# A four-layer graph network with expert layers: streams of constant products in nineteen places of TensorE's program

## The reference

```python
edge_index = jnp.stack([src, dst])
x = x + _L0_gnn_ref(_layernorm(x), edge_index, ...)     # mean over neighbours, 2 products, batch norm, relu
x = x + _L0_ffn_ref(_layernorm(x)[None], ...)[0]        # causal attention, 8 experts, softmax gate
x = x + _L1_gnn_ref(_layernorm(x), edge_index, ...)     # 2 masked attention layers, 2 batch norms each
x = x + _L1_ffn_ref(_layernorm(x)[None], ...)[0]        # 8 experts, top 2, inner width 1024
x = x + _L2_gnn_ref(_layernorm(x), edge_index, ...)     # 4 bases, weights by node, row norm
x = x + _L2_ffn_ref(_layernorm(x)[None], ...)[0]        # 8 experts, top 2, inner width 128
x = x + _L3_gnn_ref(_layernorm(x), edge_index, ...)     # normalised convolution, batch norm, gelu
x = x + _L3_ffn_ref(_layernorm(x)[None], ...)[0]        # 8 experts, top 2, gated, inner width 1536
```

## Time and profile before

| | |
|---|---|
| median of 3 runs | 1766.1 us (1761.97 to 1770.35) |
| the profiled execution's own time | 1765.15 us |
| its span | 1763.3 us |
| TensorE busy | 1551.2 us, 88% of the span |
| VectorE busy | 1252.9 us, 71% |
| ScalarE busy | 936.8 us, 53% |
| mean granted TensorE clock over the span | 0.933 of full speed |

### The profile page before, as it was taken

How to read it: one execution, slowest core, us unless ns; L and a number is a source line. 1 busy time by engine, 2 the same in 40 slices (tenths; PEclk the granted TensorE clock), 3 DMA queues, 4 the chain that set the end, 5 groups by cost and what they waited for, 6 DMA issues and landing times. The chain is left out here.

```text
span 1763.3 us, 25730 instructions
## 1 busy us (share of the span) xinstructions
PE 1551.2 (88%) x8459; PEld 1243.9 (71%) x8459; DVE 1252.9 (71%) x2075; ACT 936.8 (53%) x1590; POOL 248.5 (14%) x250
## 2 busy tenths in 40 slices
PE   6687999998996999568999957798689999999998
PEld 6667766786884887446878835584478888888886
DVE  7863664247574476558999967444579999999998
ACT  1123355433561364126999825431258878778774
POOL 2200542001120022023000030100072000000003
PEclk9988899899998999868999979799889999999999
DMA  9001000003101001224683140001325508955003
GB/s 306 28 1 48 1 1 1 13 1 132 49 2 36 1 1 62 96 64 144 243 316 137 39 157 1 0 1 71 145 71 233 232 24 327 364 225 232 18 20 98
DMA packets 42461, 173.57 MB, mean 98 GB/s; under 512 B 10219, under 2 KB 10472, under 8 KB 26905
## 3 DMA queue, kind: packets, MB, share of 16 engines
q1 hardware_dynamic: 28822, 153.94, 23.2%
q0 software_dynamic: 8960, 10.29, 2.2%
q10 hardware_dynamic: 4608, 8.39, 1.2%
HBM read 275.74 MB, written 19.51 MB: 167 GB/s over the span
## 5 line engine op out<-in xcount | busy, mean ns | idle before, releaser
L665 POOL DMA_INDIRECT sb_W<-slots_out,sb_slus x20 | 27.6, 1382 | 609.7 <-DMA slots_out<-sb_rC 604.2
L1388 ACT ACTIVATE sb_rF<-sb_rF,sb_nmx 125x625 f32<-125x625 f32 (+4 forms) x120 | 89.5, 746 | 45.0 <-DVE sb_nmx L1886 44.9
L357 DVE TENSOR_TENSOR sb_rA_r<-sb_W,sb_rA_r 128x1024 fp32r<-128x1024 f32 x68 | 83.3, 1225 | 12.2 <-ACT sb_rA_r L1487 12.2
L614 POOL TENSOR_TENSOR sb_rstd<-sb_ve,sb_half 125x5 f32<-125x5 f32 (+1 forms) x17 | 19.0, 1116 | 513.9 <-DVE sb_ve L1807 248.0
L736 PE MATMUL bank<-sb_ident,sb_XN 125*128 125x125 f32 x160 | 31.2, 382 | 65.0 <-DVE sb_XN L1833 65.0
L1886 DVE CUSTOM_DVE_ANT_0 sb_rF<-bank,sb_rG 125x625 f32<-125x625 f32 x80 | 61.5, 807 | 36.0 <-PE bank L833 35.2
L357 DVE TENSOR_TENSOR sb_XT_r<-sb_W,sb_XT_r 128x1024 fp32r<-128x1024 f32 x68 | 82.8, 1218 | 0.1
L357 DVE TENSOR_TENSOR sb_rB_r<-sb_W,sb_rB_r 128x1024 fp32r<-128x1024 f32 x68 | 82.8, 1218 | 0.0
L1487 ACT ACTIVATE sb_rA_r<-sb_W 128x1024 fp32r<-128x1024 f32 x68 | 71.4, 1050 | 17.8 <-DMA sb_W<-in_w_m 15.3
L1129 PE MATMUL bank<-sb_rA 125*125 125x313 bf16 x400 | 60.5, 315 | 21.9 <-DVE sb_rA L2212 18.7
L736 PEld LDWEIGHTS bank<-sb_ident,sb_XN 125*128 125x128 f32 x160 | 29.0, 208 | 67.4 <-DVE sb_XN L1833 67.3
(11 more groups left out here) (497 smaller groups left out, 4873.2 us busy)
## 6 DMA issues: line engine op xcount, KB each, us to landing
sb_W<-in_w_m SPq DMA_DIRECT2D x204, 1024.0 KB
sb_rDE<-in_w_m SPq DMA_DIRECT2D x17, 1024.0 KB
sb_rC<-slots_in SPq DMA_DIRECT2D x34, 256.0 KB, 2.7
sb_W<-in_w_g SPq DMA_DIRECT2D x8, 1024.0 KB, 4.9
slots_out<-sb_rC ACTq DMA_DIRECT2D x32, 256.0 KB, 2.1
slots_in<-sb_rC SPq DMA_DIRECT2D x1, 4608.0 KB, 14.4
sb_W<-in_w_a SPq DMA_DIRECT2D x4, 1024.0 KB, 30.5
sb_W<-in_w_m SPq DMA_DIRECT2D x2, 2048.0 KB, 18.6
```

Of the source, the lines that this page charges most:

```text
L357: eng.tensor_tensor(lo, src[:, HALF * h:HALF * (h + 1)], hi.bitcast(F32), ALU.subtract).then_inc(split(r, p, h, b, "lo")[0], 1)
L614: pool.tensor_tensor(dst, src, half8[0:src.shape[0], :].broadcast_to([src.shape[0], k]), ALU.pow).then_inc(S("pow"), 1)
L665: pool.indirect_dma_start(out=G[r][k][:, t], out_offset=None, in_=YS[0:P * KEPT], in_offset=bass.IndirectOffsetOnAxis(ap=slus[:, k, t:t + ...
L1388: act.activation(SM[:, s % 4, 0:kn], SM[:, s % 4, 0:kn], ACT.Exp, scale=-1.0, bias=nmx[:, s:s + 1], accum_out=dens[:, s:s + 1]).then_inc(S ...
```

## The change

A function `keep(b, n)` is added. It issues n float32 products of `ones` (128x128) with one column of `ones` repeated over 512 columns into bank b. Nobody reads the result. It is called in nineteen places of the program's course (15 calls in the code, some in a loop or a function called several times), 112 products in all, always where TensorE's next instruction waits for another engine. Because the stream writes a bank, four of the calls have a wait of their own in front that says the bank has been read: `h_done` for the batch norms, `ag_done` in graph layer 2. In the diff the first call stands in `routed_feats` (expert layers 1, 2 and 3), the second in the first block of `block_loop(1)`, and the two behind `project` in the loop over graph layer 1's two attention layers.

```diff
+            def keep(b, n):
+                for _ in range(n):
+                    pe.matmul(bank[:, b, :], ones[:], ones[:, 0:1].broadcast_to([P, D]), start=True, stop=True)
...
                 logit_rows(r)
+                keep(5, 4)
...
                         pe.wait_ge(S("b2_done"), T)
                         turn(0, b)
+                        keep(7, 4)
                         nodes(b + 1)
...
+            pe.wait_ge(S("h_done"), 8)
+            keep(7, 3)
             to_rows(HB, S("rows_full"), S("bn_out"), 0)
+            keep(7, 2)
...
+            keep(7, 3)
             pe.wait_ge(S("msk_act"), 2 * T)
...
             mixture(0)
+            keep(5 + (UNITS - 1) % 3, 7)
             ln_to_feats(3)
...
                 project([(Wo, OT)], S("g_wo_full"))
                 pe.wait_ge(S("ld_gf"), layer * 16 + 16)
+                pe.wait_ge(S("h_done"), layer * 16 + 16)
+                keep(7, 3)
...
+                pe.wait_ge(S("h_done"), layer * 16 + 24)
+                keep(7, 6)
                 pe.wait_ge(S("g_x2"), layer * 2 + 2)
                 pe.wait_ge(S("g_x2v"), layer * 2 + 2)
             to_rows(XT, S("rows_full"))
+            keep(7, 14)
...
             block_loop(1)
+            keep(7, 15)
             ln_to_feats(5)
...
+            pe.wait_ge(S("ag_done"), 9)
+            keep(0, 17)
             routed_feats(6, 7, 2)
...
             mixture(2)
+            keep(5 + (UNITS - 1) % 3, 3)
...
+            pe.wait_ge(S("h_done"), LAYERS * 16 + 16)
+            keep(7, 4)
             to_rows(HB, S("rows_full"), S("bn_out"), 4)
+            keep(7, 6)
             routed_feats(8, 9, 3)
             feats_ready(9)
             slots(3)
+            keep(5, 4)
             block_loop(3)
```

## The result

The changed kernel takes 1744.3 us (median of 4 runs, 1743.42 to 1746.73) against 1768.2 us for the kernel before (4 runs, 1761.97 to 1771.53): a ratio of 0.987, 95% interval 0.985 to 0.989. The forecast was 1742 us. On two other chips the changed kernel took 1746.3 and 1746.8 us, at ratios of 0.989 and 0.990.

What follows compares the result with a forecast made beforehand. Work at half clock behind TensorE's pauses was taken to stand on the path; halving its time where waited for summed to 23.0 us, so 1765.15 - 23.0 = 1742.2 us. Own range 1733 to 1752; 1728 to 1757 holds 8 in 10.

Steps and rivals of the forecast that it cites:

- The price of a product: Each product of the added streams: taken as 0.87 us at full clock, bounded above by some 1.75 us at half clock.
- the idle times left: Pauses filled by streams: 3.5 us left at expert layer 1, 1.8 behind `block_loop(1)`, 2.7 behind graph layer 2.
- Rests of 2.5 to 3.5 us as an even chance: Idle rests around streams: up to 1.9 us counted as keeping the clock, 2.5 to 3.5 us an even chance or worse.
- Graph layer 1: Inner products behind its pauses: full instead of half clock saves 2.4 us in the first layer, 3.0 in the second.
- The next layer's products: Graph layer 1, behind the second batch norm: mean gain 1.9 us, 1.0 if the clock falls ahead of the stream.
- Graph layer 0, 4.6 us: Graph layer 0 into attention 0: 25 transposes save 1.9 us, tiny products and transposes 2.0, `heads` 0.7.
- Expert layer 1, 1.9 us: Expert layer 1: `slots` ahead of `block_loop(1)` 1.0 us, that loop's second block 0.6, gate 0.3.
- `first_nodes` gives nothing, since the second block waits: Ahead of `block_loop(1)`: no gain from `first_nodes`, as the second block waits for GpSimd's and the DMAs' way through HBM.
- Expert layer 2 and the last loop: Expert layer 2's transposes 0.8 us at four in ten, first products of `router(2)` 1.7, ahead of the last loop 3.9.
- The first rival: All streams hold the clock and every chance becomes one: 33 us gained, 1732 us; chance 0.17.
- the second (1757): The clock falls in the rests all the same; only rests of 1.6 us and less pay: 8 us, 1757 us; chance 0.10.
- the third: The stream itself is slow, constants not counted as work or repeated column streaming badly: 1830 or 1797 us; chance 0.06.

Runs made afterwards that it cites:

- the run with the earlier start: Against the changed kernel, the stream of graph layer 1's second batch norm writes the first bank, starts at once and has 8 products instead of 6: 1746.6 us.

## Why the prediction was right, and where it wasn't

The mechanism held throughout: half clock behind pauses was the cost, the streams run at full clock, and only work that is waited for gave something. The last block loop is unchanged, as said. Against the terms of the sum:

- **The price of a product**, 0.87 us: right. The three longest streams show it, thirty records in 13.09 us (0.87 us a product) behind `block_loop(1)`, and the idle times left are those of the list:

```profile
743.62 3.61 PE L747 MATMUL bank<-sb_ones 128*128 128x512 f32 x8
750.70 1.51 PE L736 MATMUL bank<-sb_ident,sb_XN 125*128 125x125 f32 x6 [3.46 <-DVE sb_XN L1858]
...
1014.10 13.09 PE L747 MATMUL bank<-sb_ones 128*128 128x512 f32 x30
1029.38 4.03 PE L736 MATMUL bank<-sb_ident,sb_XN 125*128 125x125 f32 x20 [2.18 <-DVE sb_XN L1858]
...
1077.87 14.92 PE L747 MATMUL bank<-sb_ones 128*128 128x512 f32 x34
1095.44 2.47 PE L736 MATMUL bank<-sb_ident,sb_XN 125*128 125x125 f32 x20 [2.65 <-DVE sb_XN L1858]
```

  3.46, 2.18 and 2.65 us, for 3.5, 1.8 and 2.7 expected.
- **Rests of 2.5 to 3.5 us as an even chance**: right as a chance. 3.46 and 2.18 us were followed by a fall, 2.65 wasn't; of the two rests of 2.5 us ahead of the streams in graph layer 1's second batch norms the first was (565.63), the second wasn't. Over the three traces of the changed kernel, two of the six rests of 2.5 us were followed by a fall, none of the three of 2.65 (the same rest was in the run with the earlier start), and all three of 3.46. Between 1.9 and 2.5 us I had no price; the one rest there in the first trace, 2.18 us, was followed by a fall.
- **Graph layer 1**: 2.3 us for the first inner products (2.4 said) and 2.9 for the second (3.0). The next layer's products gave 3.1 and began 2.1 us late: 1.0, the figure given for a fall there. The mean of 1.9 was of the two cases; the first trace has the lower. In the second trace of the changed kernel the clock held there, and from the inner products to the next layer it took 17.3 us instead of 19.0, the 1.7 us that the prediction gave for the fall.
- **Graph layer 0, 4.6 us**: the term that failed. The transposes gave 1.6 (1.9 said), all the rest 0.6 instead of 2.7: the rest of 1.7 us and the tiny products behind it didn't hold, the clock fell at 176.5 us in them, and the products at 184.07 ran at 0.55. I priced 2.7 of it against the text's own reservation that I "can't hold" that trickle at full clock. The run with two more products in each closed that rest and gained 5.1 us in the same part, so the 4.6 us were there for a longer stream.
- **Attention 0 and expert layer 0**, counted at nothing, lost 2.3 us. The only stream there lies in the closing pause; the clock fell at other places, and from 290 to 350 us its mean was 0.80 instead of 0.86. The prediction had no term for stretches whose falls move. The three traces of the changed kernel have 207.7 to 210.7 us, 208.4 before.
- **Expert layer 1, 1.9 us**: 4.0. In the changed kernel the clock stays up from 791 us on, in the kernel before from 814 on; the fall at 804 that hit the second block is gone. My step "`first_nodes` gives nothing, since the second block waits" was only partly right: `nodes` waits 0.90 us instead of 4.46 us for the table, and starts 9.5 us earlier than before, of which 7.4 had been gained ahead of the layer. The 4.0 is also in part luck of this execution: the other two traces of the changed kernel have a fall at 798 and at 801 us again, and gained 0.7 and 2.0 us in this part.
- **Expert layer 2 and the last loop**: 1.6 for 0.8, since the rest of 2.65 us was kept, and 6.4 for 5.7 together up to and with `first_nodes`. The chain ahead of the last loop shows it, to be set beside the earlier trace rows:

```profile
1261.39 1.49 PE bank L986 x12
...
1266.07 1.41 DVE sb_W L2027 x5
1267.52 4.75 PE bank L1064 x40
```

  `slots` 1.49 for 2.74 us, `first_nodes` 4.75 for 7.38, each where TensorE is waited for; between them VectorE.

So the total was right to some 2 us with two terms 2.3 us too high against one 2.1 too low and smaller ones: the mechanism was right, and that the sum came so close is in part luck, since these misses cancel. By the spans the three traces of the changed kernel gained 21.7, 20.8 and 18.2 us. The first rival (1732) lost through the falls named; the second (1757) through the kept rests; the third has its mechanism shown by the eight rows, and its condition, that products of constants aren't counted, is refuted by ones and by zeros.

By the Trainium skill, page "TensorE: Matmul & The Clock Gate", section "Why this matters for your kernels", gaps under about 3 us should have been kept. The rows disagree again: 2.18 and 2.51 us were followed by half clock, and 2.65 us wasn't.

## What to carry to other kernels

Where the profile shows TensorE at 0.50 behind a pause, in work that the chain of waits goes through, fill the pause, or only its end, with full-size products whose result nobody reads, and size them so that they end 1 to 1.5 us ahead of the awaited event. Use all 128 rows (8 and 64 were the only other numbers tried, and both were worse), write a bank whose last reader is done early, so that the stream can start without a rest, and count half of the half-clock time that is waited for as the gain. Take the gain of each place from the distance between two instructions that both traces have, and expect a few us in the total to come and go with falls at places that nobody touched.

## What the runs showed of the hardware

- The granted clock depended on how many rows a product has, not only on TensorE being busy: in the three traces of the changed kernel (128 rows) it fell inside a stream only behind a rest of 2.5 us, with 64 rows also in others, with 8 rows it fell from 1.00 to 0.50 in the middle of 22.7 us without a gap.
- Zeros did as ones: a moving operand of zeros held the clock too, with inner products behind it in 4.48 us at 1.00 in both. The stationary operand was ones each time; other data were not streamed.
- A column that is repeated by its address streams at the rate of ordinary data: 0.87 us a float32 product of 128x512, as L1119's (ten records of either in 4.5 us).
- The same list of instructions met falls at different places in different executions: attention 0 with expert layer 0 took 207.7 to 210.7 us in the changed kernel. By the Trainium skill, the same page, section "Part 1: The HAM clock gate", the number of instructions that run at the low clock differs from run to run of one kernel; these stretches agree, and show it in the middle of a kernel too.
